# A transformer block on one core: the input loaded already turned, in place of four transposes per chunk

## The chip, the cores and the metric

The kernel runs on one core of a Trainium2 chip. The metric is the device time of one execution in microseconds (us). The kernel before took 1758.83 us, the median of three runs (1758.03 to 1759.03). A core has five engines that run their own instruction streams and meet at semaphores: TensorE (PE in the rows, its weight loads PEld), VectorE (DVE), ScalarE (ACT), GpSimd (POOL) and SyncE (SP), which here only issues DMAs.

## What is computed

The input `x` is [4, 2048, 512] in float32. Two sub-layers are added to it, cut here to what matters:

```
h  = (x - mean) / sqrt(var + eps)                   # outer layer norm
z  = layernorm(h) * ln_g + ln_b                      # inner layer norm
q, k, v = split(z @ W_qkv + b_qkv)                   # 16 heads of 32
g  = sigmoid(h @ W_gate + b_gate);  g = g / (mean(g) + eps)
q, k = relu(q*g)**2 + eps, relu(k*g)**2 + eps
for t:  kv += k_t (x) v_t;  ks += k_t                # causal linear attention
        o_t = (q_t @ kv) / (q_t @ ks + eps)
x1 = x + o @ W_proj + b_proj
y  = layernorm(x1)
out = x1 + (gelu((y @ U1) @ V1 + b1) @ U2) @ V2 + b2 # rank 128, 2048 wide
```

Both norms of the attention share one mean and one variance per row of `x`, so a row of `x`, less its mean, times a number per row is all that the gate and the q, k, v products need.

## The kernel before, in words

The 4 x 2048 rows are 64 chunks of 128 rows. Chunk number m = 4p + b is position p of batch b: the four batches take turns, each carrying its own attention state. All products with the 512-wide weights are split in three: a float32 value is a high part (`_hi`, of the reduced type fp32r) plus the rest (`_lo`), and a product is hi·hi + lo·hi + hi·lo, three matmuls (lines 795 to 797, helper `product`).

A matmul contracts over the partitions, so `z` (rows on partitions) has to be turned: four 128x128 transposes through the identity (`transpose4`, line 802) put it into the PSUM bank `ps_t`, ScalarE makes `zt_hi` from it (L447) and VectorE `zt_lo` (L575). The same helper turns queries, keys, and the second norm's `zs`.

The work is pipelined by steps written out by hand, one `step(p, b)` per engine, 64 of them and a few more to drain. Nothing schedules them: each engine does what its `step` lists, in that order. In step (p, b), n is the chunk whose gate, key, query and value products are made; c, the chunk before, has its scores, attention and projection; d, the one before that, goes through the second norm; and half of a two-chunk group goes through the feed-forward part (eight pairs of 256 columns: `h_pair`, gelu, `q_pair`, four pairs in odd steps and four in even ones). Even and odd steps differ in what else they hold: odd ones also have the results of an earlier group.

On TensorE the second half of a step reads: scores (L949), two `h_pair`s, a `q_pair`, the state's products (L962), query with state (L977), values with probs (L983), **the four transposes of the next chunk's `zs` (call `tz(Chunk(p, b + 1))`, L802)**, a `q_pair`, the two matmuls that sum keys (L1003, L1004), the projection of the attention output (`wp_hi`, `wp_lo` with `ot_hi`, `ot_lo`), two `q_pair`s. The output of L983 is split by ScalarE (`ot_hi`, L520) and then by VectorE (`ot_lo`, L712), and the projection waits for `ot_ready`, which VectorE gives after `ot_lo`.

On VectorE `x_norm` (L559) makes the next chunk's `zs` in the middle of a step, after the queries; `x_stats` (L544) and `x_moments` (L550) of the chunk after it are at the step's end. GpSimd makes the tiny numbers per row (`small_stats`, L357: six instructions on 128x1), adds biases (L384, L404), adds eps to the keys (L412) and makes `key_lo` (L419) and most of `h_lo` (L394). The output of `h_lo` is what a `q_pair` waits for. SyncE loads `x` three chunks ahead, stores results, and sends the last row of the key sums through DRAM to all partitions (`carry_rows`).

Of the kernel before, what the change touches and what calls it, by code (L numbers as in the profile page):

```python
# [67 lines left out]


# [34 lines left out]
def block_kernel(nc, x, ln_g, ln_b, w_qkv, b_qkv, w_gate, b_gate, w_proj, b_proj,  # L104
                 u1, v1, b1, u2, v2, b2, out, carry_dram):
    ctx = ExitStack()
    with ctx:
# [34 lines left out]
        xs = sb("xs", [P, 4, DM])  # L142
        x1s = sb("x1s", [P, 4, DM])
# [9 lines left out]
        stats, moments = sb("stats", [P, 4, 6]), sb("moments", [P, 4, 2])  # L153
        small = sb("small", [P, 4, 6])
# [11 lines left out]
        state = sb("state", [P, 2, 4, KT, HEAD])  # L166
# [23 lines left out]
        def state_of(c, turn=0):  # L190

            return state[:, (c.p + c.off // 4 + turn) % 2, c.slot, :, :]
# [17 lines left out]
        x_in = [sem(f"x_in{i}") for i in range(4)]  # L210
        stored = [sem(f"stored{i}") for i in range(4)]
# [56 lines left out]
        def _(sp):  # L268
            def load_x(c):
                if not c.exists:  # L270
                    return

                wait(sp, s["x1_steps"], Chunk(c.p, c.off - 4).done(3, 1))
                sp.dma_start(xs[:, c.slot, :], x[c.slot, bass.ds(c.row, P), :]).then_inc(x_in[c.slot], 16)

# [31 lines left out]
            load_x(Chunk(0, 2))  # L307
            load_tiles(range(FIRST, FIRST + 6))

            def step(p, b):  # L310
# [28 lines left out]
        def _(pool):  # L339
# [19 lines left out]
            def small_stats(c):  # L359
# [4 lines left out]
                var, r, done = moments[:, c.slot, 1:2], small[:, c.slot, :], s["x_small"]  # L364
# [4 lines left out]
                pool.wait_ge(done, c.done(6, 1))  # L369
                tiny(r[:, 1:2], r[:, 0:1], minus_half[:, :], ALU.pow, done)  # L370
                pool.wait_ge(done, c.done(6, 2))
                tiny(r[:, 2:3], r[:, 1:2], r[:, 1:2], ALU.mult, done)
                pool.wait_ge(done, c.done(6, 3))
                tiny(r[:, 3:4], r[:, 2:3], var, ALU.mult, done)
                pool.wait_ge(done, c.done(6, 4))
                tiny(r[:, 5:6], r[:, 3:4], eps_col[:, :], ALU.add, done)
                pool.wait_ge(done, c.done(6, 5))
                tiny(r[:, 4:5], r[:, 5:6], minus_half[:, :], ALU.pow, done)

            def add_bias(c):  # L380

                if c.exists:
                    pool.wait_ge(s["z_ready"], c.done())
# [13 lines left out]
            def step(p, b):  # L397
# [9 lines left out]
                if ffn.exists and b % 2 == 0 and not is_last(p):  # L407
                    h_tail(ffn, pairs[0])
                if n.exists:
# [3 lines left out]
                        .then_inc(s["key_ready"], 1)  # L413
                if ffn.exists and not is_last(p):
# [22 lines left out]
        def _(act):  # L437
# [6 lines left out]
            def z_head(c):  # L444
                if c.exists:
                    act.wait_ge(s["tz_done"], c.done())
                    E.activation(zt_hi[:, :, :].rearrange(flat), ps_t[:, :], ACT.Copy)\  # L447
                        .then_inc(s["zt_hi_ready"], 1)
# [84 lines left out]
        def _(dve):  # L533
            E = nc.vector

            def x_stats_wait(c):

                if c.exists:
                    dve.wait_ge(x_in[c.slot], c.dmas())
                    wait(dve, s["x_small"], Chunk(c.p, c.off - 4).done(6, 6))  # L540
# [5 lines left out]
            def x_moments(c):  # L546


                if c.exists:
                    E.bn_aggr(moments[:, c.slot, :], stats[:, c.slot, :]).then_inc(s["x_stats"], 1)  # L550

            def x_norm(c):

                if c.exists:
                    dve.wait_ge(s["x_small"], c.done(6, 2))
                    before = Chunk(c.p, c.off - 3)
                    if before.exists:
                        dve.wait_ge(s["tx_done"], before.done())
                    E.tensor_scalar(zs[:, :], xs[:, c.slot, :], moments[:, c.slot, 0:1], small[:, c.slot, 1:2],  # L559
                                    ALU.subtract, ALU.mult).then_inc(s["z_ready"], 1)  # L560

# [480 lines left out]
```

## Time and profile before

| | |
|---|---|
| runs | 1758.83 us median (1758.03 to 1759.03) |
| the profiled execution, its own time | 1757.7 us |
| its span, first to last instruction | 1755.6 us |
| mean granted TensorE clock | 0.997 of full |
| TensorE / VectorE / GpSimd / ScalarE busy | 98% / 79% / 47% / 39% |
| a pair of steps in the middle | 53.2 us |

The 2.1 us between the profiled execution's own time and its span lie around the span. A row of the timeline gives start and duration in us, the engine, the line of the kernel, the operation, output and inputs, and, in square brackets, how long the engine had been idle and what it was released by. Matmuls are pipelined: a 128x512 one lasts 0.39 us from start to end and the next starts 0.23 us after it.

### The profile page before, as it was taken

What the parts mean: (1) busy time and instruction counts of PE and PEld (TensorE: products, weight loads), DVE (VectorE), ACT (ScalarE), POOL (GpSimd) and SP (SyncE); (2) the same over time, 40 slices, a digit from 0 to 9 for tenths busy, and PEclk for the clock granted to TensorE, in tenths of its full rate; (3) what the DMA queues carried; (4) which work ended last, traced back from release to release, by engine and by line L of the source; (5) the groups of instructions that cost most, each with busy time, mean ns of one, the idle gap of its engine ahead of it and who ended that gap; (6) DMA issues with size and microseconds to landing.
All of it is one profiled execution on the core that took longest, in us unless ns stands there. A gap on an engine that the chain in (4) does not pass through costs nothing.

```text
span 1755.6 us, 39773 instructions
## 1 busy us (share of the span) xinstructions
PE 1722.4 (98%) x16729; PEld 1458.9 (83%) x16729; DVE 1385.1 (79%) x2222; ACT 676.4 (39%) x1242; POOL 825.7 (47%) x1027
## 2 busy tenths in 40 slices
PE   7899999999999999999999999999999999999997
PEld 4688888888888888888888888888888888888876
DVE  7877878877878877787788788778788778878775
ACT  4243343443434333433433433434433434344332
POOL 3354445444545544544544554544454445455440
PEclk9999999999999999999999999999999999999999
DMA  6101010011010011010011010010100110100000
GB/s 212 35 19 37 26 37 26 26 37 37 26 37 25 26 37 37 26 37 26 25 37 32 31 28 29 31 37 26 37 25 26 37 38 25 37 25 26 31 20 25
DMA packets 34720, 61.41 MB, mean 35 GB/s; under 512 B 3864, under 2 KB 6448, under 8 KB 34544
## 3 DMA queue, kind: packets, MB, share of 16 engines
q1 hardware_dynamic: 33680, 57.31, 9.9%
q8 instruction: 133, 2.18, 0.5%
q10 hardware_dynamic: 864, 1.57, 0.3%
q14 instruction: 43, 0.35, 0.1%
HBM read 41.96 MB, written 16.91 MB: 34 GB/s over the span
## 4 chain that ended last, share of the span: by engine, by line
PE 93%; DVE 1%; ACT 0%; issue 0%; POOL 0%; DVEq 0%
PE wide L795 18%; PE wide L797 18%; PE wide L796 18%; PE wide L802 7%; PE ps_h L795 4%; PE wide L949 4%; PE wide L983 4%; PE ps_h L796 3%; PE ps_q L795 3%; PE ps_h L797 3%; PE ps_q L796 3%; PE ps_q L797 3%; PE wide L977 2%; PE ps_q L962 1%; PE ps_h L1004 1%; PE ps_h L1003 1%
## 5 line engine op out<-in xcount | busy, mean ns | idle before, releaser
L394 POOL TENSOR_TENSOR h_lo<-h_full,h_hi 128x512 fp32r<-128x512 f32 x244 | 314.5, 1289 | 418.9 <-DVE h_hi L620 418.9
L795 PE MATMUL wide<-wx_hi,zt_hi 128*128 128x512 f32 x1024 | 415.2, 405 | 4.4 <-DVE zt_lo L575 3.6
L797 PE MATMUL wide<-wx_hi,zt_lo 128*128 128x512 f32 x1024 | 405.7, 396 | 0.0
L796 PE MATMUL wide<-wx_lo,zt_hi 128*128 128x512 f32 x1024 | 405.1, 396 | 0.0
L475 ACT ACTIVATE h_full<-ps_h,cols 128x256 f32<-128x256 f32 x512 | 204.0, 474 | 128.5 <-PE ps_h L797 128.1
L797 PEld LDWEIGHTS wide<-wx_hi,zt_lo 128*128 128x128 f32 x1024 | 192.8, 188 | 46.3
L795 PEld LDWEIGHTS wide<-wx_hi,zt_hi 128*128 128x128 f32 x1024 | 193.6, 189 | 42.5 <-DVE zt_lo L575 4.4
L796 PEld LDWEIGHTS wide<-wx_lo,zt_hi 128*128 128x128 f32 x1024 | 193.5, 189 | 37.4 <-issue 0.7
L357 POOL TENSOR_TENSOR small<-moments,eps_col 128x1 f32<-128x1 f32 x128 | 25.8, 201 | 395.7 <-DVE moments L764 326.4
L620 DVE CAST h_hi<-h_full 128x512 fp32r<-128x512 f32 x256 | 163.9, 640 | 35.5 <-ACT h_full L475 33.9
L698 DVE TENSOR_TENSOR probs<-wide,causal 128x2048 f32<-128x2048 f32 x64 | 146.6, 2291 | 50.2 <-PE wide L949 50.2
L486 ACT ACTIVATE query_t<-wide 128x512 f32<-128x512 f32 x64 | 38.4, 599 | 343.9 <-PE wide L802 343.9
L795 PE MATMUL ps_h<-pt_hi,v_hi 128*128 128x256 f32 x512 | 154.0, 301 | 1.4 <-DVE pt_lo L680 0.9
L795 PE MATMUL ps_q<-h_hi,u_hi 128*128 128x256 f32 x512 | 150.0, 293 | 0.4
L796 PE MATMUL ps_h<-pt_lo,v_hi 128*128 128x256 f32 x512 | 144.9, 283 | 0.0
L796 PE MATMUL ps_q<-h_lo,u_hi 128*128 128x256 f32 x512 | 144.4, 282 | 0.0
L797 PE MATMUL ps_h<-pt_hi,v_lo 128*128 128x256 f32 x512 | 144.1, 281 | 0.0
L797 PE MATMUL ps_q<-h_hi,u_lo 128*128 128x256 f32 x512 | 143.4, 280 | 0.0
L501 ACT ACTIVATE key_t<-wide 128x512 f32<-128x512 f32 x64 | 38.3, 598 | 211.8 <-PE wide L802 211.8
L357 POOL TENSOR_TENSOR small<-small,minus_half 128x1 f32<-128x1 f32 x192 | 107.7, 561 | 15.1
L384 POOL TENSOR_TENSOR xs<-xs,bias_proj 128x512 f32<-128x512 f32 x64 | 110.2, 1722 | 5.1 <-DMA bias_out<-L_ffn_b 5.1
L795 PEld LDWEIGHTS ps_h<-pt_hi,v_hi 128*128 128x128 f32 x512 | 97.0, 189 | 12.3 <-DVE pt_lo L680 1.1
(150 smaller groups left out, 3798.0 us busy)
## 6 DMA issues: line engine op xcount, KB each, us to landing
xs<-L_attn_x SPq DMA_DIRECT2D x64, 256.0 KB, 2.7
out<-x1s SPq DMA_DIRECT2D x64, 256.0 KB, 2.1
key_sums<-carry_rows SPq DMA_DIRECT2D x60, 256.0 KB, 3.1
x1s<-L_attn_W_gate SPq DMA_DIRECT2D x4, 256.0 KB, 4.1
x1s<-L_ffn_U SPq DMA_DIRECT2D x4, 256.0 KB, 3.3
carry_rows<-key_sums SPq DMA_DIRECT2D x64, 2.0 KB
probs<-L_attn_W_qkv SPq DMA_DIRECT2D x3, 256.0 KB, 5.7
bias<-L_attn_b_qkv ACTq DMA_DIRECT2D x3, 256.0 KB, 6.8
```

The lines of the kernel that those rows point to most:

```text
L357: E.tensor_tensor(out_, a, b, op).then_inc(sem_, 1)
L384: E.tensor_tensor(xs[:, c.slot, :], xs[:, c.slot, :], bias_proj[:, :], ALU.add)\
L394: E.tensor_tensor(h_lo[:, i % SLOTS, :], h_full[:, i % SLOTS, :], h_hi[:, i % SLOTS, :].bitcast(F32), ALU.subtract).then_inc(s["h_lo_ready ...
L475: last = E.activation(h_full[:, i % SLOTS, a * GROUP:(a + 1) * GROUP], ps_h[i % 2][:, a * GROUP:(a + 1) * GROUP], ACT.Gelu_apprx_tanh, bia ...
L620: E.tensor_copy(h_hi[:, i % SLOTS, :], h_full[:, i % SLOTS, :]).then_inc(s["h_hi_ready"], 1)
L698: E.tensor_tensor(probs[:, :, :].rearrange("p j (k t) -> p (j k) t", k=KT), scores.rearrange("p (g t) -> p g t", g=blocks), causal.unsquee ...
L795: E.matmul(ps, wh, mh, start=start and i == 0, stop=False)
L796: E.matmul(ps, wh, ml, start=False, stop=False)
L797: mm = E.matmul(ps, wl, mh, start=False, stop=stop and i == last)
L802: mm = E.transpose(ps_t[:, k * P:(k + 1) * P], src[:, k * P:(k + 1) * P], ident[:, :])
L949: mm = E.matmul(ps_scores[j][:, ft * P:(ft + 1) * P], key_t[rows, ft, :], query_t[rows, ft, :], start=True, stop=True, tile_position=(HEAD ...
L983: mm = E.matmul(ps_out[j][ft * HEAD:(ft + 1) * HEAD, 0:P], values[:, c.half, h * HEAD:(h + 1) * HEAD], probs[:, j, ft * P:(ft + 1) * P], s ...
```

## The change

The host gives the kernel a second copy of `x` in which, in each chunk, the 512 features are on partitions and the 128 rows along the free dimension. SyncE loads its tile `xt` for each chunk but the first. The mean of each row is needed along the free dimension on every partition: the 128 means go to DRAM as a column (`means_out`) and come back as one row broadcast to all partitions (`means_in`, tile `rows`). GpSimd subtracts (`center`), and `zt_hi` and `zt_lo` are made from `xt` in SBUF rather than from PSUM. The division by the standard deviation, which `x_norm` did, moves to where the gate is read out of PSUM (a factor per row), and the key, query and value read-outs use the one of both norms as they did. `x_norm` and the call `tz` are gone but for chunk 0. The statistics of chunk n + 2 move from the end of the step to `x_norm`'s place. `small_stats` has five instructions, no longer six. The attention states take five tiles in turn in place of eight.

```diff
+            def means_out(c):
+                if c.exists:
+                    sp.wait_ge(s["x_stats"], c.done(2, 2))
+                    sp.dma_start(rows_dram[c.slot, :].rearrange("(t a) -> t a", a=1), small[:, c.slot, 2:3])\
+                        .then_inc(rows_out[c.slot], 16)
+            def means_in(c):
+                if c.exists:
+                    sp.wait_ge(rows_out[c.slot], c.turned())
+                    wait(sp, s["z_ready"], Chunk(c.p, c.off - 2).done())
+                    sp.dma_start(rows[:, c.half, :],
+                                 rows_dram[c.slot, :].rearrange("(a t) -> a t", a=1).broadcast_to([P, P]))\
+                        .then_inc(rows_in[c.slot], 16)
@@ SyncE, step(p, b): after the stores of an odd step, before the carried key sums
+                means_out(Chunk(p, b + 2))
+                means_in(Chunk(p, b + 2))
@@ SyncE, load_x
+                if c.p or c.off:
+                    wait(sp, s["zt_ready"], Chunk(c.p, c.off - 2).done())
+                    sp.dma_start(xt[:, c.half, :, :].rearrange(flat), x_turned[c.slot, c.row // P, :, :])\
+                        .then_inc(xt_in[c.slot], 16)
@@ GpSimd
+            def center(c):
+                if not c.exists:
+                    return
+                mine = xt[:, c.half, :, :]
+                pool.wait_ge(xt_in[c.slot], c.turned())
+                pool.wait_ge(rows_in[c.slot], c.turned())
+                E.tensor_tensor(mine, mine, rows[:, c.half, :].unsqueeze(1).broadcast_to([P, KT, P]),
+                                ALU.subtract).then_inc(s["z_ready"], 1)
@@ GpSimd, step
                 add_bias(n)
-                if ffn.exists and b % 2 == 0 and not is_last(p):
-                    h_tail(ffn, pairs[0])
+                if ffn.exists and b % 2 == 0:
+                    center(Chunk(p, b + 1))
+                    if not is_last(p):
+                        h_tail(ffn, pairs[0])
...
+                if b % 2 or not ffn.exists:
+                    center(Chunk(p, b + 1))
@@ ScalarE, z_head
-                    act.wait_ge(s["tz_done"], c.done())
+                    if c.p or c.off:
+                        act.wait_ge(s["z_ready"], c.done())
+                        act.wait_ge(s["value_done"], Chunk(c.p, c.off - 1).done())
+                        turned = xt[:, c.half, :, :].rearrange(flat)
...
@@ VectorE
-            x_norm(Chunk(0, 0))
+            dve.wait_ge(s["x_stats"], 2)
+            E.tensor_scalar(zs[:, :], xs[:, 0, :], small[:, 0, 2:3], None, ALU.subtract).then_inc(s["z_ready"], 1)
...
-                    E.tensor_tensor(gate[:, :], ps_b[:, :], bias[:, GATE, :], ALU.add)\
+                    dve.wait_ge(s["x_small"], n.done(5, 2))
+                    E.scalar_tensor_tensor(out=gate[:, :], in0=ps_b[:, :], scalar=small[:, n.slot, 1:2],
+                                           in1=bias[:, GATE, :], op0=ALU.mult, op1=ALU.add)\
                         .then_inc(s["gate_evac"], 1)
...
-                x_norm(Chunk(p, b + 1))
...
+                ahead = Chunk(p, b + 2)
+                x_stats_wait(ahead)
+                x_stats(ahead)
...
+                x_moments(ahead)
@@ TensorE, step
                     mm.then_inc(s["ot_done"], 1)
-                tz(Chunk(p, b + 1))
@@ the state
-            return state[:, (c.p + c.off // 4 + turn) % 2, c.slot, :, :]
+            return state[:, (4 * c.p + c.off + BATCHES * (turn - 1)) % (BATCHES + 1), :, :]
```

On TensorE, after the values' product of one step, the order before is this; `ident,zs` with `x4` is the turned input, the `ps_q` rows are a `q_pair`, `wp` with `ot` is the projection.

```order
L983 MATMUL wide<-probs,values 32x128 x16
L802 MATMUL wide<-ident,zs 128x128 x4
L795 MATMUL ps_q<-h_hi,u_hi 128x256
L796 MATMUL ps_q<-h_lo,u_hi 128x256
L797 MATMUL ps_q<-h_hi,u_lo 128x256
L795 MATMUL ps_q<-h_hi,u_hi 128x256
L796 MATMUL ps_q<-h_lo,u_hi 128x256
L797 MATMUL ps_q<-h_hi,u_lo 128x256
L1003 MATMUL ps_h<-key_hi,causal 128x512
L1004 MATMUL ps_h<-key_lo,causal 128x512
L795 MATMUL wide<-wp_hi,ot_hi 128x512
```

The same place in the changed kernel, whose line numbers are higher:

```order
L1014 MATMUL wide<-probs,values 32x128 x16
L835 MATMUL ps_q<-h_hi,u_hi 128x256
L836 MATMUL ps_q<-h_lo,u_hi 128x256
L837 MATMUL ps_q<-h_hi,u_lo 128x256
L835 MATMUL ps_q<-h_hi,u_hi 128x256
L836 MATMUL ps_q<-h_lo,u_hi 128x256
L837 MATMUL ps_q<-h_hi,u_lo 128x256
L1033 MATMUL ps_h<-key_hi,causal 128x512
L1034 MATMUL ps_h<-key_lo,causal 128x512
L835 MATMUL wide<-wp_hi,ot_hi 128x512
```

The four transposes are gone, and nothing stands in their place between the values' product and the projection.

On GpSimd, an even step from the second norm's bias to the last `h_lo`, before:

```order
L404 TENSOR_TENSOR x1s<-x1s,bias_out 128x512
L384 TENSOR_TENSOR xs<-xs,bias_proj 128x512
L394 TENSOR_TENSOR h_lo<-h_full,h_hi 128x512
L412 TENSOR_TENSOR keys<-keys,eps_col 128x512
L419 TENSOR_TENSOR key_lo<-keys,key_hi 128x512
L394 TENSOR_TENSOR h_lo<-h_full,h_hi 128x512 x3
```

and in the changed kernel:

```order
L443 TENSOR_TENSOR x1s<-x1s,bias_out 128x512
L423 TENSOR_TENSOR xs<-xs,bias_proj 128x512
L414 TENSOR_TENSOR xt<-xt,rows 128x512
L433 TENSOR_TENSOR h_lo<-h_full,h_hi 128x512
L453 TENSOR_TENSOR keys<-keys,eps_col 128x512
L462 TENSOR_TENSOR key_lo<-keys,key_hi 128x512
L433 TENSOR_TENSOR h_lo<-h_full,h_hi 128x512 x3
```

The centring stands ahead of the first `h_lo`; in odd steps it stands behind the keys' eps and ahead of the first `h_lo`.

On VectorE, the middle of an odd step, from the queries to the scores, before:

```order
L611 SCALAR_TENSOR_TENSOR queries<-queries,gate_scale,gate 128x512
L615 SCALAR_TENSOR_TENSOR queries<-queries 128x512
L559 TENSOR_SCALAR zs<-xs,moments,small 128x512
L680 TENSOR_TENSOR pt_lo<-wide,pt_hi 128x256
L688 SCALAR_TENSOR_TENSOR values<-wide,small,bias 128x512
```

and in the changed kernel:

```order
L654 SCALAR_TENSOR_TENSOR queries<-queries,gate_scale,gate 128x512
L658 SCALAR_TENSOR_TENSOR queries<-queries 128x512
L724 TENSOR_TENSOR pt_lo<-wide,pt_hi 128x256
L595 BN_STATS stats<-xs 128x6
L601 BN_AGGR small<-stats 128x2
L738 SCALAR_TENSOR_TENSOR values<-wide,small,bias 128x512
```

The norm of the next chunk has gone, and the statistics of the chunk after it have come from the step's end; in an even step they stand there ahead of the first `h_hi`.

## Rows read from the trace of the kernel before

**Rows 1.** The page: busy time, share of the span and instructions by engine.
```profile
PE 1722.4 (98%) x16729; PEld 1458.9 (83%) x16729; DVE 1385.1 (79%) x2222; ACT 676.4 (39%) x1242; POOL 825.7 (47%) x1027
```
**Rows 2.** Stretches: length, busy time and count by engine, clock, DMA share, GB/s.
```profile
159.00:1690.00 1531.00, 1531.00 (x15099) 1304.85 (x15092) 1222.11 (x1960) 596.13 (x1090) 749.93 (x920) 1.00 0.10 31
```
**Rows 3.** Timeline of an even step in the middle, values' product to projection.
```profile
822.03 1.08 PE L983 MATMUL wide<-probs,values 128*32 128x128 f32 x32
...
823.04 0.66 PE L802 MATMUL wide<-ident,zs 128*128 128x128 f32 x4
823.18 0.60 ACT L520 ACTIVATE ot_hi<-wide 128x512 fp32r<-128x512 f32 x1 [1.74 <-PE wide L983]
...
823.46 0.36 PE L795 MATMUL ps_q<-h_hi,u_hi 128*128 128x256 f32 x1
...
823.81 0.69 DVE L712 TENSOR_TENSOR ot_lo<-wide,ot_hi 128x512 fp32r<-128x512 f32 x1 [0.54 <-ACT ot_hi L520]
...
824.48 0.39 PE L1004 MATMUL ps_h<-key_lo,causal 128*128 128x512 f32 x1
824.56 0.19 PEld L795 LDWEIGHTS wide<-wp_hi,ot_hi 128*128 128x128 f32 x1
...
824.95 0.40 PE L796 MATMUL wide<-wp_lo,ot_hi 128*128 128x512 f32 x1
```
**Rows 4.** Timeline of the last attention step, which has no input transposes.
```profile
1721.30 1.08 PE L983 MATMUL wide<-probs,values 128*32 128x128 f32 x32
...
1723.08 0.69 DVE L712 TENSOR_TENSOR ot_lo<-wide,ot_hi 128x512 fp32r<-128x512 f32 x1 [0.18 <-ACT ot_hi L520]
...
1723.82 0.51 PE L795 MATMUL wide<-wp_hi,ot_hi 128*128 128x512 f32 x1 [0.54 <-DVE ot_lo L712]
...
1724.16 0.39 PE L796 MATMUL wide<-wp_lo,ot_hi 128*128 128x512 f32 x1
```
**Rows 5.** Timeline of startup: VectorE's first norm and split, TensorE's first product.
```profile
7.49 0.55 DVE L559 TENSOR_SCALAR zs<-xs,moments,small 128x512 f32<-128x512 f32 x1 [1.01 <-POOL small L357]
...
10.36 0.69 DVE L575 TENSOR_TENSOR zt_lo<-wide,zt_hi 128x512 fp32r<-128x512 f32 x1
...
11.10 0.80 PE L795 MATMUL wide<-wx_hi,zt_hi 128*128 128x512 f32 x1 [1.89 <-DVE zt_lo L575]
```
**Rows 6.** Timeline of startup, ScalarE: the gate's weights and the turned input.
```profile
6.27 2.54 ACT L456 ACTIVATE wx_hi<-x1s 128x512 fp32r<-128x512 f32 x4 [1.74 <-DMA x1s<-L_attn_W_gate]
9.24 0.60 ACT L447 ACTIVATE zt_hi<-wide 128x512 fp32r<-128x512 f32 x1 [0.43 <-PE wide L802]
```
**Rows 7.** Timeline of GpSimd, an even step; the last row is an odd one's.
```profile
811.42 1.75 POOL L384 TENSOR_TENSOR xs<-xs,bias_proj 128x512 f32<-128x512 f32 x1
816.95 1.29 POOL L394 TENSOR_TENSOR h_lo<-h_full,h_hi 128x512 fp32r<-128x512 f32 x1 [3.77 <-DVE h_hi L620]
...
819.97 1.29 POOL L419 TENSOR_TENSOR key_lo<-keys,key_hi 128x512 fp32r<-128x512 f32 x1 [0.74 <-ACT key_hi L514]
821.71 1.28 POOL L394 TENSOR_TENSOR h_lo<-h_full,h_hi 128x512 fp32r<-128x512 f32 x1 [0.44 <-DVE h_hi L620]
...
846.53 1.29 POOL L394 TENSOR_TENSOR h_lo<-h_full,h_hi 128x512 fp32r<-128x512 f32 x1 [6.49 <-DVE h_hi L620]
```
**Rows 8.** Timeline of VectorE, the same even step.
```profile
815.82 0.54 DVE L559 TENSOR_SCALAR zs<-xs,moments,small 128x512 f32<-128x512 f32 x1
816.44 0.43 DVE L620 CAST h_hi<-h_full 128x512 fp32r<-128x512 f32 x1
...
821.93 1.34 DVE L620 CAST h_hi<-h_full 128x512 fp32r<-128x512 f32 x1
```
**Rows 9.** GpSimd's bias add: count, shortest, median, longest in ns.
```profile
L384 POOL TENSOR_TENSOR xs<-xs,bias_proj x64: 1277/1746/1795, 24.9 to 1684.5; 128x512 f32<-128x512 f32 x64
```
**Rows 10.** VectorE by line: the statistics of `x`, busy, mean ns, idle before.
```profile
L544 DVE BATCH_NORM_STATS2 stats<-xs 128x6 f32<-128x512 f32 x64 | 44.4, 694 | 6.2 <-DMA xs<-L_attn_x 4.1
```
**Rows 11.** The page's DMA issues: KB each, median us to landing.
```profile
key_sums<-carry_rows SPq DMA_DIRECT2D x60, 256.0 KB, 3.1
```

More of the change, by code:

```diff
@@ L67, in dmas, with turned @@
         return self.p * 16 + 16 * (self.off // 4 + 1)
+    def turned(self):
+        return self.dmas() - (16 if self.slot == 0 else 0)
 class Group:
@@ L142, in block_kernel @@
         xs = sb("xs", [P, 4, DM])
+        xt = sb("xt", [P, 2, KT, P])
+        rows = sb("rows", [P, 2, P])
         x1s = sb("x1s", [P, 4, DM])
@@ L210, in block_kernel @@
         x_in = [sem(f"x_in{i}") for i in range(4)]
+        xt_in = [sem(f"xt_in{i}") for i in range(4)]
+        rows_out = [sem(f"rows_out{i}") for i in range(4)]
+        rows_in = [sem(f"rows_in{i}") for i in range(4)]
         stored = [sem(f"stored{i}") for i in range(4)]
@@ L539, in x_stats_wait @@
                     dve.wait_ge(x_in[c.slot], c.dmas())
-                    wait(dve, s["x_small"], Chunk(c.p, c.off - 4).done(6, 6))
+                    before = Chunk(c.p, c.off - 4)
+                    wait(dve, s["x_small"], before.done(5, 5))
+                    if before.exists:
+                        wait(dve, rows_out[c.slot], before.turned())
             def x_stats(c):
@@ L549, in x_moments @@
                 if c.exists:
[L550 to L560, printed above, removed]
-            E.memset(state[:, 0, :, :, :].rearrange("p b k n -> p (b k n)"), 0.0).then_inc(s["state_zero"], 1)
+                    E.bn_aggr(small[:, c.slot, 2:4], stats[:, c.slot, :]).then_inc(s["x_stats"], 1)
+            E.memset(state[:, :, :, :].rearrange("p b k n -> p (b k n)"), 0.0).then_inc(s["state_zero"], 1)
             def first_stats(m):
@@ L574, in z_tail @@
                     dve.wait_ge(s["zt_hi_ready"], c.done())
-                    E.tensor_tensor(zt_lo[:, :, :].rearrange(flat), ps_t[:, :],
+                    turned = xt[:, c.half, :, :].rearrange(flat) if c.p or c.off else ps_t[:, :]
+                    E.tensor_tensor(zt_lo[:, :, :].rearrange(flat), turned,
                                     zt_hi[:, :, :].rearrange(flat).bitcast(F32), ALU.subtract)\
@@ L681, in step @@
                         .then_inc(s["pt_ready"], 1)
+                ahead = Chunk(p, b + 2)
+                x_stats_wait(ahead)
+                x_stats(ahead)
+                if ahead.exists:
+                    dve.wait_ge(s["x_stats"], ahead.done(2, 1))
+                x_moments(ahead)
                 if ffn.exists and b % 2 == 0:
@@ L759, in step @@
                     wait(dve, s["x1_small"], d.done(2, 2))
-                ahead = Chunk(p, b + 2)
-                x_stats_wait(ahead)
-                x_stats(ahead)
-                if c.exists:
                     E.bn_aggr(moments1[:, :], stats1[:, :]).then_inc(s["x1_steps"], 1)
-                if ahead.exists:
-                    dve.wait_ge(s["x_stats"], ahead.done(2, 1))
-                if c.exists:
                     dve.wait_ge(s["x1_small"], c.done(2, 2))
-                    after = Chunk(p, b + 1)
-                    if after.exists:
-                        dve.wait_ge(s["tz_done"], after.done())
-                    elif d.exists:
+                    if d.exists:
                         dve.wait_ge(s["tx_done"], d.done())
+                    elif not c.p and not c.off:
+                        dve.wait_ge(s["tz_done"], 1)
                     E.tensor_scalar(zs[:, :], x1s[:, c.slot, :], moments1[:, 0:1], small1[:, 1:2],
                                     ALU.subtract, ALU.mult).then_inc(s["z1_ready"], 1)
-                x_moments(ahead)
                 if ffn.exists and b % 2 == 0:
@@ L821, in bias_products @@
                         .then_inc(s["stage_bias"], 1)
-            def tz(c):
-                if not c.exists:
-                    return
-                pe.wait_ge(s["z_ready"], c.done())
-                before = Chunk(c.p, c.off - 2)
-                if before.exists:
-                    pe.wait_ge(s["probs_ready"], before.done())
-                transpose4(zs, s["tz_done"])
-            tz(Chunk(0, 0))
+            pe.wait_ge(s["z_ready"], 1)
+            transpose4(zs, s["tz_done"])
             def h_pair(g, i):
@@ L873, in step @@
                     pe.wait_ge(s["den_steps"], c.done(6, 6))
-                    if n.exists:
-                        pe.wait_ge(s["zt_ready"], n.done())
-                    else:
+                    if d.exists:
                         pe.wait_ge(s["probs_ready"], d.done())
```

44 lines of the change are left out of this document (25 added, 19 removed).

## The prediction

> **What bounds the kernel now.** I read the page first. TensorE is busy for 98% of the span, VectorE for 79%, GpSimd for 47% [rows 1]. A share of busy time doesn't say where TensorE's end is set, so the next view is the table of stretches: from 159 to 1690 us TensorE has no idle time at all, 1531.00 of 1531.00 us at the full granted clock [rows 2]. In this part, 58 steps (1531 us in pairs of 53.2 us), only what shortens TensorE's own stream shortens the kernel, as long as no wait appears in it. All that TensorE idles, 1755.6 less 1722.4 or 33.2 us, lies before it and behind it, and most of it is startup and drain.
>
> The third view is the timeline around what is removed, and it decides the case. In the even step shown, the values' product starts at 822.03. The four transposes of the input start at 823.04 and the next matmul at 823.46, so they hold TensorE for 0.42 us [rows 3]. Beside them runs a chain that the projection needs: ScalarE starts `ot_hi` at 823.18, 1.15 us behind the start of the values' product, VectorE makes `ot_lo` from 823.81 to 824.50, and the weight load of the projection starts at 824.56, 0.06 us after that. That load should have come earlier: a load elsewhere in the stream starts together with the matmul ahead of it, here L1004 at 824.48. It came 0.08 us late, so the projection's load was already let go by `ot_lo`. The matmul stream hides it, because the load is short and the array was still working. TensorE shows no idle time there, but it has no slack either.
>
> **The transposes removed.** 63 times 0.42 us is 26.5 us, and that is the gain if nothing else were waited for. But between the values' product and the projection there are then only a `q_pair` and the key sums: from 823.46 to the start of L1004 at 824.48 is 1.02 us, and 0.23 more to its successor. Moved to 823.04, the projection would be due at 824.29, while the chain, which starts at the end of the values' product and holds no transposes, still ends in a weight load at 824.56. The kernel before has a step that shows the new layout: in its last attention step no next chunk exists, so the `q_pair` follows the values' product directly. There `ot_lo` starts 1.78 us after the start of the values' product, as in the middle; TensorE idles 0.54 us for it, starts the first projection matmul at +2.52 and the second at +2.86 (1724.16 less 1721.30) [rows 4]. In the middle the second starts at +2.92 (824.95 less 822.03) [rows 3]. So a step gains 2.92 less 2.86, 0.06 us, and not 0.42. Over 58 steps this is 3.5 us. Both ends for this term: 0, if the restart after a wait costs a little more than there, and 26.5 if the chain could be hurried. I take 3.5, since rows 4 are this very place.
>
> **Startup.** VectorE's first `zs` waited 1.01 us for GpSimd's power, which centring alone doesn't need [rows 5]. `zs` comes 1 us earlier; the four weight tiles that VectorE makes between it and `zt_lo` take 2.3 us (8.04 to 10.36), and would now run from about 7.1 to 9.5, if ScalarE delivers them: its four end at 8.8, and its `zt_hi`, which idled 0.43 us for the transposes, then follows at 8.8 to 9.4 [rows 6]. `zt_lo` starts at about 9.5 in place of 10.36, so the first product is 0.9 us earlier. Against it, the 256 KB of the first `xt` are put between weight tiles that are being loaded; the bounds are 0.9 saved and, from the 3.1 us that a 256 KB DMA takes to land [rows 11], about 2 lost. The order of TensorE's work up to 35 us is long enough to hide a tile that is 1 us late, so I take 0.9 saved.
>
> **What is added, and its cover.** *GpSimd* gets one 128x512 subtraction per chunk. The nearest row is the bias add with two operands in SBUF, 1.28 to 1.80 us, mostly 1.75 [rows 9]. In an even step it starts behind that add, at 813.17, and GpSimd would otherwise idle 3.77 us before `h_lo` at 816.95; in an odd step the idle time is 6.49 us [rows 7]. So it is over before `h_lo`'s turn. *VectorE* loses the norm (0.54 us) in the middle and gets the statistics there, 0.69 us and a short aggregate, from the step's end [rows 8, 10], so the `h_hi` of 816.44 comes about 0.3 us later. Another 0.2 comes from the two engines being in each other's way: the `h_hi` of 821.93 takes 1.34 us in place of 0.43 because GpSimd's `h_lo` runs from 821.71 to 822.99, and ends 0.28 us behind it [rows 7, 8]. The centring ends at about 814.9 and holds up one operation on the queries in the same manner. Together about 0.5 us on the first `h_lo`. Behind it on GpSimd stand the keys' eps, `key_lo` and the second `h_lo`, which idled 0.44 us before its start at 821.71 [rows 7]. So 0.5 us is swallowed but for 0.06, and the `q_pair` that waits for that `h_lo` has 0.27 us in hand (824.29 against 824.56 above). I cost it at nothing; without that cover each us more costs TensorE one us in every even step.
>
> The Trainium skill, "SBUF — State Buffer", section "Who interferes with whom", says that GpSimd and a VectorE operation with two SBUF inputs or in a two-port mode exclude each other for a whole instruction, and that the second "fully blocks". The 1.34 us above agree. By that rule `zt_lo` too, which now has both inputs in SBUF, would be held up by the `h_lo` that starts at 823.35; it is needed only some 4 us later, so the sum stays as it is.
>
> *The read-out of the gate* becomes a multiply and add, about 0.1 us longer, but the end of the step has lost 0.69 us of statistics ahead of it. *SyncE* gets three DMAs per chunk. The means leave at about 817 and come back after two trips, at most 2 x 3.1 us [rows 11], by 824; the centring that needs them is 16 us later, in the next step. SyncE itself is held only for the first trip, until about 820.5, and its next task, the carried key sums, waits for the product L1004 at 824.48 [rows 3]. Cost nothing. *The five states* are no wait: the slot written was read a step earlier.
>
> **The sum.** 3.5 + 0.9 = 4.4 us less. The profiled execution took 1757.7 us, 1.1 below the median of the runs. From it: 1753.3; on the scale of the runs, 1758.83 - 4.4 = 1754.4 us, 0.25% less. A difference under about 0.2%, 3.5 us, can't be told from none.
>
> **Rivals.** (1) *The whole stream shortens*: 26.5 + 0.9 us, 1731.4. For it speaks that TensorE never idles in 1531 us; against it, that the last attention step shows the wait, with the same chain to the hundredth of a us. The Trainium skill, "Perfetto Trace Analysis", section "Identifying the Most-Contended Engine", says to optimize the engine with the highest occupancy first; taken alone that points to this case. The trace bears it out only in that TensorE is that engine. Chance 5%.
>
> (2) *Nothing to be told*: the restart after the wait eats the 0.06 us, or startup loses what it won. Gain 0 to 3.5 us, 1755.3 to 1758.8. For it: the gain per step is a difference of two numbers read to 0.01 us, and rows 4 have fewer waits around them. Against: this is the same code. Chance 30%, of which a few per cent on the side of slower.
>
> (3) *GpSimd is late in even steps, and the kernel is slower.* The place is the second `h_lo`. If the centring takes over 2.3 us there, or holds up two operations of VectorE, the delay passes the 0.44 and 0.27 us in hand, and `ot_lo`, which stands behind an `h_hi` that has to wait for that `h_lo`, is late as well: it has 0.54 us [rows 3]. It decides from a delay of about 0.75 us on the first `h_lo` on. At 1.1 us each of some 30 even steps loses 0.35, 10 us: 1758.8 + 10 - 4 = 1765. For it: my 0.5 already uses up the first cover. Against: no bias add is over 1.80 us. Chance 12%.
>
> **Chances.** The forecast 53%, (1) 5%, (2) 30%, (3) 12%. The forecast's own range is 1751 to 1757. Faster by over 0.2% is most of the forecast and (1): 50%. Within 0.2%: the rest of the forecast and most of (2): 35%. Slower: (3) and what is left of (2), 15%. The range for 8 in 10 leaves out (1) and the worse half of (3): 1748 to 1763.
>
> **What would show it.** In the profile after, TensorE's stream should have, in each step, 0.5 us in place of 0.23 from the start of the second key-sum matmul to the start of the projection's first; 0.39 of them are that matmul, so about 0.1 us a step, 6 us in all, should show as idle, released by `ot_lo`, and a pair of steps should last 53.1 us. The centring should take 1.3 to 1.8 us with its end well before the first `h_lo`; the second `h_lo` of even steps should start as before relative to the values' product. A pair of steps of 52.3 us would mean (1). A wait of TensorE for `h_lo`, or an `ot_lo` that starts later than 1.78 us behind the values' product, would mean (3). A first product later than 11.1 us would make the startup term wrong.

## The result, and the profile after

The changed kernel took 1838.19 us, the median of six runs (1829.81 to 1840.41), beside 1758.88 us for the kernel before on the same chip (1757.7 in its profiled execution): a ratio of 1.0441, 95% interval 1.0418 to 1.0465. It is 79 us slower. The forecast was 1754.4, the range ended at 1763, and "slower" had 15%. The profiled execution of the kernel after took 1829.8 us, its span is 1828.1.

The page of the kernel after, in the order of its sections: busy time by engine, all DMA packets, the queue that brings instructions, and the chain that ended last.
```profile
PE 1745.9 (96%) x16477; PEld 1446.4 (79%) x16477; DVE 1330.5 (73%) x2159; ACT 674.7 (37%) x1242; POOL 886.6 (48%) x1026
...
DMA packets 61937, 82.09 MB, mean 45 GB/s; under 512 B 14952, under 2 KB 25600, under 8 KB 61760
...
q8 instruction: 131, 2.15, 0.9%
...
PE 85%; DVE 6%; ACT 3%; issue 3%; another core or an unknown queue 1%; DMA 1%; POOL 1%; SPq 0%; DVEq 0%
```
The same lines of the page before, but for the first, which is in [rows 1].
```profile
DMA packets 34720, 61.41 MB, mean 35 GB/s; under 512 B 3864, under 2 KB 6448, under 8 KB 34544
...
q8 instruction: 133, 2.18, 0.5%
...
PE 93%; DVE 1%; ACT 0%; issue 0%; POOL 0%; DVEq 0%
```
TensorE has 252 instructions fewer than in [rows 1] and is busy for 23.5 us more. It idles 82.2 us (1828.1 less 1745.9) where it idled 33.2. In the chain "issue", time in which an engine waited for nothing that the profile shows, has gone from 0% to 3%, and "an unknown queue" is new. And one line has changed that no edit was about: q8 moves about the same (131 packets, 2.15 MB, where it was 133 and 2.18), and its packets take 0.9% of the time of the DMA engines in place of 0.5%.

The table of stretches of the kernel after, columns as in [rows 2]: the middle, and then three stretches around one stall.
```profile
159.00:1690.00 1531.00, 1487.14 (x14364) 1238.36 (x14358) 1120.36 (x1817) 570.99 (x1049) 774.91 (x884) 0.99 0.14 41
...
350.00:354.00 4.00, 2.18 (x83) 1.49 (x85) 2.05 (x4) 0.34 (x1) 2.69 (x3) 0.95 0.05 4
354.00:356.00 2.00, 2.00 (x27) 1.61 (x19) 0.14 (x1) 0.77 (x2) 0.00 (x0) 0.50 0.00 0
356.00:358.00 2.00, 2.00 (x10) 1.73 (x10) 2.00 (x4) 0.34 (x1) 0.44 (x1) 0.74 0.10 33
```
Where [rows 2] had no idle time in 1531 us, there are now 43.9. After a stall of some 2 us the granted clock falls to 0.50, the lower of its two levels, 1.2 GHz, and TensorE shows as fully busy, but the matmuls of a `q_pair` start 0.21 us apart (355.50 and 355.71), not 0.12 as before the stall. So a stall can be paid twice: against an undisturbed version of this kernel (e4 below, span 1753.1, TensorE busy 1717.2) the 75.0 us are 46.3 of idle time and 28.7 of longer busy time. The clock explains about 12 of the 28.7: it stood at 0.50 for 41.0 us of this span and for 17.1 of e4's, and half of the difference is lost. The rest was not broken down.

What TensorE waited for, in the kernel after: us in total, times, longest.
```profile
PE wide L835 <- DVE ot_lo L762: 16.5, 18, 2.3
PE wide L1014 <- issue: 15.5, 18, 2.3
PE wide L1008 <- issue: 13.4, 15, 2.6
```
The timeline of one stalled step after; the last number in brackets is the idle time before an instruction.
```profile
1127.28 1.08 PE L1014 MATMUL wide<-probs,values 128*32 128x128 f32 x32
...
1129.38 0.40 PE L1034 MATMUL ps_h<-key_lo,causal 128*128 128x512 f32 x1
...
1130.74 0.60 ACT L568 ACTIVATE ot_hi<-wide 128x512 fp32r<-128x512 f32 x1 [4.05 <-remote]
...
1131.37 0.69 DVE L762 TENSOR_TENSOR ot_lo<-wide,ot_hi 128x512 fp32r<-128x512 f32 x1 [2.86 <-ACT ot_hi L568]
...
1132.11 0.80 PE L835 MATMUL wide<-wp_hi,ot_hi 128*128 128x512 f32 x1 [2.33 <-DVE ot_lo L762]
```
`ot_lo` is named as what TensorE waited for, but it isn't the cause. The values' product had ended at 1128.36; ScalarE should have started `ot_hi` then and started it at 1130.74, after 4.05 us of idle time that ended by nothing the profile finds on this core ("remote"). Another stall is inside TensorE's own stream, and needs no other engine:
```profile
350.92 0.41 PE L1014 MATMUL wide<-probs,values 128*32 128x128 f32 x5
352.22 0.27 PE L1014 MATMUL wide<-probs,values 128*32 128x128 f32 x1 [0.89 <-issue]
353.42 1.77 PE L1014 MATMUL wide<-probs,values 128*32 128x128 f32 x26 [0.93 <-issue]
```
These are 32 matmuls of one group, with no wait between them in the kernel. TensorE ran five, stopped, ran one, stopped. I took this for a lack of instructions; a packet of q8 runs from 351.38 to 354.77, across both stalls.

Some microseconds ahead of these stalls SyncE sends the means, and it is itself held there. Its rows in the kernel after:
```profile
1121.75 0.33 SPq L291 DMA_DIRECT2D turned_rows<-small  x1
...
1130.06 0.33 SPq L298 DMA_DIRECT2D rows<-turned_rows  x1
```
The second DMA waits for the receipt of the first: 8.3 us for 512 bytes; over the 63 chunks the median is 7.9. The 131 packets of q8 in the same trace, taken one by one: 51 take over 2.3 us, 3.25 in the median, and every one of these begins 2.0 to 8.9 us behind the issue of a write of the means; the other 80 take 1.04 in the median, and only five of them begin in that stretch. In the kernel before all 133 take 1.7 us or less, 1.13 in the mean. I call them instruction fetches below.

Where no fetch is slow, a step is as forecast. An undisturbed one of the kernel after:
```profile
1522.12 1.08 PE L1014 MATMUL wide<-probs,values 128*32 128x128 f32 x32
...
1523.90 0.69 DVE L762 TENSOR_TENSOR ot_lo<-wide,ot_hi 128x512 fp32r<-128x512 f32 x1 [0.55 <-ACT ot_hi L568]
...
1524.64 0.50 PE L835 MATMUL wide<-wp_hi,ot_hi 128*128 128x512 f32 x1
...
1524.98 0.39 PE L836 MATMUL wide<-wp_lo,ot_hi 128*128 128x512 f32 x1
```
`ot_lo` at +1.78 and the second projection matmul at +2.86, the hundredths of [rows 4]. The theory from here on, called T: the 128 writes of 4 bytes delay instruction fetches, engines run dry, and nothing else is wrong with the change.

### The profile page after: what moved, and what is told of

The parts are those of the page before. It is cut to its first block, busy times and chain, and to the rows that moved or that the text cites. A ratio compares the mean times of both kernels' runs of the same rounds, so it can differ in the third digit from the quotient of the medians.

```text
span 1828.1 us, 39520 instructions
## 1 busy us (share of the span) xinstructions
PE 1745.9 (96%) x16477; PEld 1446.4 (79%) x16477; DVE 1330.5 (73%) x2159; ACT 674.7 (37%) x1242; POOL 886.6 (48%) x1026
## 3 DMA queue, kind: packets, MB, share of 16 engines
q8 instruction: 131, 2.15, 0.9%
## 4 chain that ended last, share of the span: by engine, by line
PE 85%; DVE 6%; ACT 3%; issue 3%; another core or an unknown queue 1%; DMA 1%; POOL 1%; SPq 0%; DVEq 0%
PE wide L835 17%; PE wide L837 17%; PE wide L836 17%; PE wide L1014 4%; PE wide L842 4%; PE ps_h L835 4%; PE wide L980 3%; PE ps_q L835 3%; PE ps_h L836 3%; PE ps_h L837 3%; PE ps_q L836 3%; PE ps_q L837 3%; PE wide L1008 2%; DVE ot_lo L762 1%; ACT ot_hi L568 1%
## 5 line engine op out<-in xcount | busy, mean ns | idle before, releaser
L663 DVE CAST h_hi<-h_full 128x512 fp32r<-128x512 f32 x256 | 151.3, 591 | 34.4 <-ACT h_full L523 34.4
L387 POOL TENSOR_TENSOR small<-moments,eps_col 128x1 f32<-128x1 f32 x64 | 12.3, 192 | 290.2 <-DVE moments L810 290.2
L835 PE MATMUL wide<-wp_hi,ot_hi 128*128 128x512 f32 x256 | 109.7, 429 | 18.3 <-DVE ot_lo L762 16.5
L387 POOL TENSOR_TENSOR small<-small,minus_half 128x1 f32<-128x1 f32 x192 | 119.9, 624 | 15.0
L835 PEld LDWEIGHTS ps_q<-h_hi,u_hi 128*128 128x128 f32 x512 | 97.3, 190 | 19.8 <-issue 15.5
```

What stands on the lines that cost most here:

```text
L387: E.tensor_tensor(out_, a, b, op).then_inc(sem_, 1)
L663: E.tensor_copy(h_hi[:, i % SLOTS, :], h_full[:, i % SLOTS, :]).then_inc(s["h_hi_ready"], 1)
L835: E.matmul(ps, wh, mh, start=start and i == 0, stop=False)
```

## The experiments

**e1_no_means: neither of the two DMAs of the means.** The changed kernel, with the first two lines in both `means_out` and `means_in`, and the subtraction of zeros in `center`:
```diff
-                if c.exists:
+                if False:
...
-                pool.wait_ge(rows_in[c.slot], c.turned())
+            E.memset(rows[:, :, :].rearrange("p a t -> p (a t)"), 0.0)
...
-                        wait(dve, rows_out[c.slot], before.turned())
+                        pass
```
The last lines take out VectorE's wait for the write of four chunks earlier, which no longer happens.

> The changed kernel without the two DMAs that turn the means: GpSimd subtracts a tile of zeros, all else is kept (the kernel leaves out the subtraction of the mean in the product's input). Theory T (the 128 writes of 4 bytes into DRAM hold up the instruction fetches that come in the next microseconds, and engines run dry): back to the predicted 1753 to 1757 us, mean time of an instruction packet about 1.15 us, a pair of steps 53.1 us. Rival L (the second 256 KB load per chunk is what delays the fetches): stays at 1825 to 1840 us. Rival G (the centring on GpSimd and its port): stays over 1800 us.

Measured: 1755.39 us, ratio 0.9979 (0.9969 to 0.9988). The whole loss is gone, and what is left is the forecast: 3.6 us less than the kernel before, where 4.4 were predicted.

**e2_out_only: the means are written and never read.** The same edit for `means_in` alone, with the zeros; the write and VectorE's wait stay.

> The changed kernel with the means written to DRAM but never read back; GpSimd subtracts zeros (the subtraction of the mean is left out). Theory T: the 4-byte writes alone do it, 1825 to 1840 us, instruction packets as slow as in the changed kernel, 1.9 us in the mean. Rival R (it is the broadcast read of the means, 128 packets of 512 bytes, that is in the way): 1753 to 1757 us.

Measured: 1812.37 us, ratio 1.0311 (1.0292 to 1.0329). The write alone costs 57 us against e1; 51 of its 131 fetches are slow, as many as with the read. But the whole change costs 26 us more than this (1838.19), so the read or SyncE's wait for the receipt has a part. The expectation of 1825 to 1840 was too high for that.

**e3_before_tiny: the kernel before, and one write of 128 x 4 bytes per chunk that nobody reads.**
```diff
+                e = Chunk(p, b + 1)
+                if e.exists:
+                    sp.wait_ge(s["z_ready"], e.done())
+                    sp.dma_start(extra_dram[e.slot, :].rearrange("(t a) -> t a", a=1), moments[:, e.slot, 0:1], allow_slow_non_contiguous=True).then_inc(extra_out[e.slot], 16)
...
+                sp.wait_ge(extra_out[i], 16 * POSITIONS - (16 if i == 0 else 0))
```


> The kernel before plus one DMA per chunk that writes the 128 means of the next chunk, 4 bytes each, to DRAM in the middle of the step, and nothing that reads them. Theory T: slower by as much as the changed kernel was off its forecast, some 50 to 85 us, 1810 to 1845 us. Rivals L, G and R: no change, 1757 to 1761 us.

Measured: 1821.85 us, ratio 1.0364 (1.0349 to 1.038). The last line of the edit stands behind all steps. So a DMA that no engine waits for before the kernel's end, put into the unchanged kernel, costs it 63 us. What TensorE waited for most there, and q8 on its page (0.5% before):
```profile
PE wide L983 <- issue: 21.5, 17, 2.7
...
q8 instruction: 133, 2.18, 0.9%
```
48 of its 133 fetches are slow. Of the 63.3 us between the spans, 34.0 are idle time of TensorE and 29.3 longer busy time. This shows that the write is the cause, without any other part of the change.

It doesn't show the whole path. TensorE stalls for over 0.3 us 24 times between 100 and 1690 us, 30.0 us in all, and every stall begins 5.6 to 7.3 us behind the issue of such a write. In 16 of them (18.0 us) a slow fetch runs during the stall or has ended in the 2 us before it; in 8 (12.0 us) there is none. In the kernel after, 42 of 43 stalls begin 5.5 to 9.3 us behind a write, and 28 of the 43 (30.6 of 42.4 us) go with a slow fetch. No run delays the fetches in another way. That the write causes the stalls is shown; that it does so by slow fetches is likely for a good part of them and not shown for the rest.

**e4_bounce: the whole change, the means sent through one row of SBUF.**
```diff
+        row1 = sb("row1", [1, P])
...
-                    sp.dma_start(rows_dram[c.slot, :].rearrange("(t a) -> t a", a=1), small[:, c.slot, 2:3])\
-                        .then_inc(rows_out[c.slot], 16)
+                    sp.dma_start(row1[0:1, :], small[:, c.slot, 2:3]).then_inc(row1_in[c.slot], 16)
+                    sp.wait_ge(row1_in[c.slot], c.turned())
+                    sp.dma_start(rows_dram[c.slot:c.slot + 1, :], row1[0:1, :]).then_inc(rows_out[c.slot], 16)
```


> The changed kernel, complete, but the column of means first goes into one row of SBUF (128 packets of 4 bytes, none to DRAM) and from there to DRAM in one piece of 512 bytes, then back as before. Theory T, if it is the small writes to DRAM: 1753 to 1757 us. If 128 packets of 4 bytes do it wherever they land: over 1800 us.

Measured: 1755.04 us, ratio 0.9979 (0.9969 to 0.9988). The output is complete, and there is one DMA more per chunk than in the change; the 128 pieces of 4 bytes are still there, but they land in SBUF. SyncE in this kernel:
```profile
815.97 0.49 SPq L293 DMA_DIRECT2D row<-small  x1
817.89 0.25 SPq L295 DMA_DIRECT2D turned_rows<-row  x1
818.99 0.34 SPq L301 DMA_DIRECT2D rows<-turned_rows  x1
```
1.9 us into SBUF, then 1.1 us for the 512 bytes to DRAM in one piece, where 128 pieces took 7.9. No fetch is slow (mean 1.13). So it is neither the count of packets nor their size alone; the pieces have to go into DRAM.

**e5, e6, e7, e9: which property of the write?** Each is e3 with the destination, or the piece, changed (e6 and e7 write from the constant tile `causal`). The list gives what each writes:
```diff
+ e5_tiny_apart     extra_dram[e.slot, :, 0:1]  <- 4 B,   each in its own 512 B
+ e9_tiny_64_apart  extra_dram[e.slot, :, 0:1]  <- 4 B,   each in its own 64 B
+ e6_before_64b     extra_dram[e.slot, :, 0:16] <- 64 B,  in a row
+ e7_before_512b    extra_dram[e.slot, :, :]    <- 512 B, in a row
```


> The kernel before plus, per chunk, the same 128 writes of 4 bytes to DRAM, but each into its own stretch of 512 bytes, in place of 512 bytes in a row. If the writes hold each other up because they fall into the same few hundred bytes: the loss falls to under a third of the 63 us of e3, below 1780 us. If each small write has its price wherever it goes: 1810 to 1835 us again.

> The kernel before plus 128 writes of 64 bytes each per chunk to DRAM, in a row (8 KB). If what costs is a write shorter than 64 bytes: no loss, 1757 to 1762 us. If every write under 512 bytes costs: 1800 to 1835 us.

> The kernel before plus 128 writes of 512 bytes each per chunk to DRAM, in a row (64 KB): the same number of packets as in e3 and 128 times the bytes. If the size of a packet is what matters: no loss, 1757 to 1762 us. If the number of packets, or the wait for them, is: 1810 us or more.

> The kernel before plus the 128 writes of 4 bytes per chunk, each into its own stretch of 64 bytes. Theory P (what costs is that several small writes go into the same 64 bytes, one after another): no loss, 1757 to 1762 us. If the place must differ by more than 64 bytes: a loss between 10 and 63 us.

Measured: e5 1759.55 us, ratio 1.0001 (0.9991 to 1.0011); e6 1759.23 us, 1.0 (0.999 to 1.001); e7 1759.51 us, 1.0003 (0.9992 to 1.0013); e9 1759.51 us, 1.0 (0.999 to 1.0011). None costs anything that can be told, and none has a slow fetch. The same 128 pieces of 4 bytes cost 63 us when sixteen of them share 64 bytes, and nothing when each has its own 64. The page of e9 gives its write:
```profile
extra_rows<-moments SPq DMA_DIRECT2D x63, 0.5 KB, 1.4
```
It has landed after 1.4 us, as in e5 and e6 (e7: 1.5). In e3 the last receipt of a write comes after 7.5 us in the median of the 31 writes whose receipts the trace holds in full. Distances between 4 and 64 bytes were not tried, so the limit lies somewhere between them.

The Trainium skill, "DMA: Bandwidth & Descriptors", section "Specifications", puts the smallest transfer for full rate at 512 bytes and says that below it "SDMA does read-modify-write". What happens here isn't explained by that size: e5, e9 and e6 lie below it too and lose nothing. What decides here is how close together the pieces land.

**e10_tiny_half: e3 with 64 partitions in place of 128.**

> The kernel before plus 64 writes of 4 bytes in a row per chunk in place of the 128 of e3 (63 us). If the writes are served one after another at some 60 ns each, the memory is held for half the time and fewer fetches fall into it: a loss of 10 to 35 us, 1769 to 1794 us. If a burst has a fixed price: about 63 us, 1822 us.

Measured: 1792.24 us, ratio 1.0187 (1.0167 to 1.0208). Half the pieces, 33 us in place of 63. 42 fetches are slow, 2.76 us in the median, and begin up to 7.6 us behind the issue of the write, where it was 8.5 in e3. Both the number and the length of the slow fetches fall.

The expectation got the loss right and its reason wrong. If pieces were served one after another at some 60 ns, 64 of them would take half the time. But the last receipt comes after 7.05 us in the median of 43 writes, hardly sooner than the 7.5 of e3; only the first comes much earlier (1.5 against 3.3 us). So between 64 and 128 pieces the time of a burst hardly changes, and why the loss is half stays open.

**e11_read_other: what the read adds.** The changed kernel, in which the broadcast reads a row of `x` in place of the means, so that a wrong row is subtracted; the write and all waits are as they were.
```diff
-                    sp.dma_start(rows[:, c.half, :],
-                                 rows_dram[c.slot, :].rearrange("(a t) -> a t", a=1).broadcast_to([P, P]))\
+                    sp.dma_start(rows[:, c.half, :], x[c.slot, c.row:c.row + 1, 0:P].broadcast_to([P, P]))\
```


> The changed kernel, but what is broadcast behind the write of the means is a row of x from DRAM, not the means themselves (so it subtracts a wrong row). e2, with no read, took 1812 us, the changed kernel 1838. If the 26 us more come from reading back the place just written: about 1812 us here. If they come from any read, or from waiting for the write before it: 1830 to 1840 us.

Measured: 1835.57 us, ratio 1.0425 (1.0395 to 1.0454). The 26 us don't come from reading the place just written. The landing time of this DMA does: 4.8 us in the kernel after, 3.1 here, 2.8 in e4; but that is no likely cause, since GpSimd waited for it for 2.1 us in all in the kernel after. Whether the 26 us are SyncE's wait for the receipt, or any read behind the write, was not told apart. The difference is also less sure than the others: the six runs of the kernel after spread over 10.6 us.

**e8_bounce_hi_first: what the transposes' time turned into.** With the loss out of the way, the question of the sum was left: 26.5 us of transposes removed, under 4 gained. e4 with the projection's eight products of `ot_hi` first, which don't need `ot_lo`. `ot_lo` is made from the bank `ps_a`, so the sum can't start there before it is read; it goes to `ps_t`, which the transposes have left:
```diff
-                    E.tensor_tensor(x1s[:, c.slot, :], ps_a[:, :], xs[:, c.slot, :], ALU.add)\
+                    E.tensor_tensor(x1s[:, c.slot, :], ps_t[:, :], xs[:, c.slot, :], ALU.add)\
...
+                        pe.wait_ge(s["x1_steps"], d.done(3, 1))
...
+                    pe.wait_ge(s["ot_hi_ready"], c.done())
+                    for k in range(KT):
+                        E.matmul(ps_t[:, :], ot_hi[:, k, :], wp_hi[:, k, :], start=k == 0, stop=False)
+                        E.matmul(ps_t[:, :], ot_hi[:, k, :], wp_lo[:, k, :], start=False, stop=False)
                     pe.wait_ge(s["ot_ready"], c.done())
...
+                    for k in range(KT):
+                        mm = E.matmul(ps_t[:, :], ot_lo[:, k, :], wp_hi[:, k, :], start=False, stop=k == KT - 1)
```


> e4 with the projection's eight products with ot_hi ahead of the four with ot_lo, so that only the latter wait for VectorE, and with its sum in the bank ps_t, which without the transposes is free. Theory W (in e4 the transposes' time turned into a wait for ot_lo): the wait goes, up to 0.36 us in each of 58 steps, 20 us: 1734 to 1738 us. Rival (another wait takes its place at once, for h_lo or probs): 1745 us or more.

Measured: 1742.15 us, ratio 0.9902 (0.9886 to 0.9919). 12.9 us less than e4, by the order of twelve matmuls and the bank that this order needs: TensorE was held by `ot_lo`. It is less than expected (1734 to 1738): a wait that had been covered comes up behind it, the `q_pair` for the `h_lo` of GpSimd, 28 times (what TensorE waited for from 159 to 1690 us in this kernel):
```profile
PE ps_q L838 <- POOL h_lo L436: 5.6, 28, 0.2
```

**e12_sums_first: e8 with the two key-sum matmuls ahead of that `q_pair`.**

> e8 with the two key-sum matmuls ahead of the q_pair that follows the values' product. In e8 that q_pair starts 1.24 us behind the values' product's start, where 1.01 was possible, and waits for an h_lo of GpSimd. With 0.45 us of key sums ahead of it the wait should go: 0.2 us in each of 58 steps, 1729 to 1733 us. Rival (the wait for ot_lo, probs or a later h_lo comes in its place): 1738 us or more.

Measured: 1734.34 us (1732.19 to 1736.78), ratio 0.9858 (0.9844 to 0.9873), 24.8 us less than the kernel before and the fastest of all, 1.3 us above the expected range. Its timeline in the same place:
```profile
815.26 1.08 PE L1018 MATMUL wide<-probs,values 128*32 128x128 f32 x32
816.27 0.51 PE L1033 MATMUL ps_h<-key_hi,causal 128*128 128x512 f32 x1
...
816.81 1.31 POOL L436 TENSOR_TENSOR h_lo<-h_full,h_hi 128x512 fp32r<-128x512 f32 x1 [0.36 <-DVE h_hi L666]
816.85 0.28 PE L838 MATMUL ps_q<-h_hi,u_hi 128*128 128x256 f32 x1
...
817.55 0.39 PE L1046 MATMUL wide<-wp_hi,ot_hi 128*128 128x512 f32 x1
817.65 1.02 DVE L621 TENSOR_TENSOR zt_lo<-xt,zt_hi 128x512 fp32r<-128x512 f32 x1
817.78 0.40 PE L1047 MATMUL wide<-wp_lo,ot_hi 128*128 128x512 f32 x1
```
The second projection matmul starts at +2.52, not +2.86. That is 0.40 less than the +2.92 of [rows 3], nearly all of the transposes' 0.42.

## Why the prediction was wrong

**The step that failed** is in the paragraph on SyncE's three DMAs: "The means leave at about 817 and come back after two trips, at most 2 x 3.1 us [rows 11]" and "Cost nothing." The bound was taken from the landing of a 256 KB DMA, as if bytes set the time. 512 bytes in 128 pieces took 7.9 us for the first trip alone, more than both trips were to take. And "cost nothing" rested on who waits for the data. Nobody did, as the centring's line in the kernel after shows (count, busy and mean; idle time before it):
```profile
L414 POOL TENSOR_TENSOR xt<-xt,rows 128x512 f32<-128x512 f32 x63 | 96.1, 1526 | 2.1 <-DMA rows<-turned_rows 2.1
```
The cost went past all semaphores: 51 of 131 instruction fetches took 3.25 us instead of about 1.1, and TensorE, ScalarE and VectorE stalled in the microseconds behind the writes, with the lower clock after some stalls. Together this was 79 us. e3 shows the write's price alone (63 us), e1 and e4 take it away; that all of it goes through the fetches is not shown. No rival had it; rival 3's sign was right and its mechanism wrong. The page of before lists instruction packets among the DMA queues (q8); I never asked what a write could do to them.

**The term for the transposes** was right: 0.06 us a step, since `ot_lo` is waited for. e1 and e4, which lack the slow write, came out 3.6 and 3.9 us below the kernel before, 4.4 forecast. e4's timeline:
```profile
821.42 1.08 PE L1017 MATMUL wide<-probs,values 128*32 128x128 f32 x32
...
823.21 0.69 DVE L765 TENSOR_TENSOR ot_lo<-wide,ot_hi 128x512 fp32r<-128x512 f32 x1 [0.55 <-ACT ot_hi L571]
...
823.53 0.40 PE L1037 MATMUL ps_h<-key_lo,causal 128*128 128x512 f32 x1
...
823.95 0.50 PE L838 MATMUL wide<-wp_hi,ot_hi 128*128 128x512 f32 x1
824.29 0.39 PE L839 MATMUL wide<-wp_lo,ot_hi 128*128 128x512 f32 x1
```
+2.87 for the second projection matmul (2.86 forecast), 0.42 us from the second key-sum matmul to the projection's first (0.5 forecast), 53.04 us for a pair of steps (53.1). What I said of its look was wrong: not 6 us of idle time, but 2.1 in the middle (its row of the stretch, below), since the projection's first matmul starts 0.42 us after one that lasts 0.40, which leaves 0.02 idle. e8 and e12 show that it was this wait.
```profile
159.00:1690.00 1531.00, 1528.89 (x14951) 1280.69 (x14951) 1188.82 (x1907) 595.45 (x1093) 806.71 (x920) 1.00 0.14 43
```

**Startup** was right to 0.15 us, in part by luck. The first product was forecast at 10.2 (11.10 less 0.9, [rows 5]). It came at 10.35 in the kernel after, where VectorE could start on `x` 0.55 us earlier than before; in e1 it came at 10.46 and in e4 at 10.85 (`x` 0.30 and 0.18 earlier), so there the term was worth 0.6 and 0.25 us. VectorE and TensorE in the kernel after:
```profile
9.61 0.68 DVE L618 TENSOR_TENSOR zt_lo<-wide,zt_hi 128x512 fp32r<-128x512 f32 x1
...
10.35 0.80 PE L835 MATMUL wide<-wx_hi,zt_hi 128*128 128x512 f32 x1 [2.74 <-DVE zt_lo L618]
```

**GpSimd** was right in the sum and too dark in detail. In an even step of e4:
```profile
810.63 1.77 POOL L417 TENSOR_TENSOR xt<-xt,rows 128x512 f32<-128x512 f32 x1
816.34 1.29 POOL L436 TENSOR_TENSOR h_lo<-h_full,h_hi 128x512 fp32r<-128x512 f32 x1 [3.94 <-DVE h_hi L666]
...
821.10 1.28 POOL L436 TENSOR_TENSOR h_lo<-h_full,h_hi 128x512 fp32r<-128x512 f32 x1 [0.43 <-DVE h_hi L666]
```
The centring takes 1.77 us here and 1.53 in the mean of the kernel after, within the 1.28 to 1.80 of [rows 9]. The first `h_lo` starts 5.08 us ahead of the values' product, exactly as in [rows 7] with [rows 3], and not 0.5 later as I had worked out; the second kept its 0.43 us. Rival 3 is refuted: e1 and e4 keep the centring and lose nothing. Behind e8 the cover of that `h_lo` did run out, but by 0.2 us and for another reason: TensorE had come forward.

**Rival 1**, the whole stream shorter, 1731.4, did not come true for this change. It is what e12 nearly reaches (1734.34) once the wait is moved as well.

**What stays open:** why the loss is 79 us with a broadcast read behind the write and 53 without (e2, e11), while as many fetches are slow; what holds up an engine in the stalls that no slow fetch goes with; and why half the pieces cost half, though their last receipt comes nearly as late (e10).

## What to carry to other kernels

Count the pieces of a DMA and where each lands, not only its bytes: a column of an SBUF tile that goes to consecutive words of DRAM is 128 writes of 4 bytes, and here it cost 63 us over 63 chunks though nobody waited for it. Send it through one row of SBUF (e4), or give each value 64 bytes of its own (e9, tried for the write alone). When engines idle for "issue" or for something "remote" while their operands are ready, compare the time of the instruction queue's packets with that of the kernel before. And before counting on time removed from a full engine, ask which chain would be due next: here it took 0.36 of 0.42 us, and two changes of order got nearly all of it back.

## What the runs showed of the hardware

- 128 writes of 4 bytes into 512 consecutive bytes of DRAM: receipt after 7.9 us in the kernel after, 7.5 in e3; the pieces themselves are on the DMA engines for about 9 ns each, and the last starts 1.0 us behind the issue. 64 such writes into 256 bytes: 7.05 us (e10). Each in its own 64 or 512 bytes: 1.4 us (e9, e5). In one piece of 512 bytes: 1.1 us (e4). That pieces which meet in the same 64 bytes hold each other up is my reading of e3 against e9; that other reads of DRAM queue behind them, of the slow fetches. The runs show both effects, not the mechanism, and not at which distance between 4 and 64 bytes it ends.
- An instruction fetch, 16 KB, takes 1.1 us at rest, and the core makes one every 13 us in this kernel (133 in 1755.6 us). Fetches of up to 1.7 us went with no stall in the middle of the kernel before; with 51 of 3.25 us TensorE idled 43.9 us there in the kernel after.
- VectorE's `zt_lo`, 0.68 us alone (37.71 us in the kernel after), takes 0.77 in e4 and 1.02 in e12, where it starts inside GpSimd's `h_lo`. It ends 0.56 and 0.55 us behind the end of `h_lo` (824.59 less 824.03; 818.67 less 818.12), and all 60 of e4 that start inside an `h_lo` end 0.54 to 0.56 behind it. So it gets on only when GpSimd is done. The Trainium skill, "SBUF — State Buffer", section "Who interferes with whom", has this as its rule; here the trace agrees, and it cost the kernel nothing.
